# A recurrent layer on one core: the fifth mix matmul issued in turn with the first decay product, into other rows of the same PSUM bank

## The reference

```python
xn = _ln(x, ln1_w, ln1_b)
sx = _token_shift(xn, state[:, i1])                       # xn of the token before, minus xn
xxx = jnp.tanh((xn + sx * maa_x) @ maa_w1)                # 256 -> 5 * 32: the five mixes
xxx = jnp.matmul(xxx.reshape(b, l, 5, 1, 32), maa_w2)     # each 32 -> 256
x5 = xn[:, :, None] + sx[:, :, None] * (maa_stack + xxx)  # five modulated inputs
w = jnp.exp(-jnp.exp(time_decay + jnp.tanh(x5[:, :, 1] @ decay_w1) @ decay_w2))
r, k, v, g = x5[3] @ Wr.T, x5[0] @ Wk.T, x5[2] @ Wv.T, silu(x5[4] @ Wg.T)
# scan over tokens: out = r . (u * k v + s);  s = k v + w * s
# then a group norm, the gate, Wo, and a gated feed-forward with a token shift of its own
```

## Time and profile before

| what | us |
|---|---|
| median of 3 runs | 780.33 (779.73 to 785.28) |
| the profiled execution, its own time | 782.66 |
| its span in the trace | 780.9 |
| busy: PE / DVE / ACT / POOL | 670.8 / 647.7 / 367.4 / 269.7 |
| of it, pass from 495 to 560 us: PE / DVE / ACT / POOL | 58.1 / 63.1 / 30.4 / 31.0 of 65 |
| mean granted clock of PE over the span | 0.952 of full |

### The profile page before, as it was taken

How to read it: one execution, slowest core, us unless ns; L and a number is a source line. 1 busy time by engine, 2 the same in 40 slices (tenths; PEclk the granted TensorE clock), 3 DMA queues, 4 the chain that set the end, 5 groups by cost and what they waited for, 6 DMA issues and landing times.

```text
span 780.9 us, 9718 instructions
## 1 busy us (share of the span) xinstructions
PE 670.8 (86%) x2736; PEld 361.8 (46%) x2736; DVE 647.7 (83%) x983; ACT 367.4 (47%) x805; POOL 269.7 (35%) x192
## 2 busy tenths in 40 slices
PE   7789999979966978898988989898898988956887
PEld 5456666656422324253453435335344442514575
DVE  2499999973457799999999999999989999899623
ACT  3478888852241245346345244644615443352342
POOL 2840000000563363353626335354443633461000
PEclk9699999999998899999999999999999999997899
DMA  2611212200290443327055151514705332350000
GB/s 69 194 55 54 67 54 61 74 14 27 61 182 0 84 82 78 65 44 161 0 108 130 32 107 38 124 26 82 161 1 107 74 60 60 66 118 0 18 9 27
DMA packets 38298, 54.17 MB, mean 69 GB/s; under 512 B 4626, under 2 KB 21154, under 8 KB 38146
## 3 DMA queue, kind: packets, MB, share of 16 engines
q1 hardware_dynamic: 36866, 50.46, 28.8%
q0 software_dynamic: 1408, 3.43, 1.3%
HBM read 16.13 MB, written 4.19 MB: 26 GB/s over the span
## 4 chain that ended last, share of the span: by engine, by line
PE 29%; DVE 26%; issue 14%; ACT 3%; DMA 1%; POOL 1%; DVEq 1%; SPq 1%; POOLq 0%; ACTq 0%
DVE state L1174 13%; PE ps_a L733 6%; PE ps_a L746 4%; PE ps_a L762 4%; PE ps_c L819 4%; PE ps_c L733 3%; PE ps_a L771 2%; DVE x L1140 2%; PE ps_att L799 1%; DVE vb L1179 1%; DVE sx L1199 1%; DVE bonus L1148 1%; DVE st L1108 1%; ACT xn L1025 1%; PE ps_a L791 1%
## 5 line engine op out<-in xcount | busy, mean ns | idle before, releaser
L658 POOL TENSOR_TENSOR x<-x,xn 128x1024 f32<-128x1024 f32 x40 | 90.0, 2251 | 236.7 <-DVE x L1140 236.7
L1174 DVE TENSOR_TENSOR_SCAN state<-ps_w,state 128x512 f32<-128x512 f32 x128 | 145.8, 1201 | 9.2 <-ACT state L940 6.2
L733 PE MATMUL ps_a<-x,wsq 128*128 128x512 f32 x256 | 119.8, 610 | 11.1 <-ACT k L990 6.0
L653 POOL TENSOR_TENSOR state<-vb,k 128x2016 f32<-128x2016 f32 x24 | 114.3, 4761 | 41.9 <-ACT k L990 18.5
L1179 DVE TENSOR_TENSOR vb<-state,r 128x2048 f32<-128x2048 f32 x32 | 110.4, 3451 | 1.7
L1140 DVE SCALAR_TENSOR_TENSOR x<-ps_a,vec,sx 128x512 f32<-128x512 f32 x80 | 57.5, 745 | 42.2 <-PE ps_a L762 32.4
L733 PEld LDWEIGHTS ps_a<-x,wsq 128*128 128x128 f32 x256 | 47.9, 193 | 72.4 <-issue 55.7
L762 PE MATMUL ps_a<-mix_t,w 128*128 128x512 f32 x128 | 64.4, 618 | 14.9 <-DVE x L1140 14.9
L296 ACT ACTIVATE probs<-ps_f,negmax 128x256 f32<-128x256 f32 x128 | 58.8, 472 | 2.0 <-DVE negmax L345 1.2
L733 PE MATMUL ps_c<-zn,wsq 128*128 128x512 f32 x64 | 35.1, 699 | 17.4 <-DVE zn L1203 17.4
L345 DVE TENSOR_REDUCE negmax<-ps_f 128x2 f32<-128x512 f32 x64 | 41.2, 686 | 8.0 <-PE ps_f L218 5.6
(11 more groups left out here) (167 smaller groups left out, 1257.6 us busy)
## 6 DMA issues: line engine op xcount, KB each, us to landing
vb<-v SPq DMA_DIRECT2D x128, 256.0 KB, 5.8
x<-in_x SPq DMA_DIRECT2D x32, 128.0 KB, 2.1
c<-in_ctx SPq DMA_DIRECT2D x32, 128.0 KB, 2.1
x_chunk<-in_x SPq DMA_DIRECT2D x8, 512.0 KB, 7.4
out<-sx SPq DMA_DIRECT2D x8, 512.0 KB, 3.0
wsq<-in_wsq POOLq DMA_DIRECT2D x1, 1024.0 KB, 5.2
wsq<-in_wsq POOLq DMA_DIRECT2D x1, 768.0 KB, 6.8
s<-in_s POOLq DMA_DIRECT2D x1, 512.0 KB, 7.8
```

The lines of the kernel that those rows point to most:

```text
L653: nc.gpsimd.tensor_tensor(st[q][:, :, :, 1:L], src[:, :, :, 0:L - 1], wide(k[p][h][:, :])[:, :, :, 0:L - 1], ALU.mult).then_inc(kv_pool, 1)
L658: nc.gpsimd.tensor_tensor(x5[j % 2][:, :, :], x5[j % 2][:, :, :], xn[:, :, 1:L1], ALU.add).then_inc(x5_ready, 1)
L733: mm = nc.tensor.matmul(bank[:, :], wsq[:, weight, c, P * o:P * o + P], src(c), start=(c == 0), stop=(c == EC - 1))
L1174: nc.vector.tensor_tensor_scan(row, w[h][:, :], row, 0.0, ALU.mult, ALU.add).then_inc(scanned, 1)
```

## The change

Four things are altered.

1. `m1` leaves `a_mix` and the list `A_ORDER`. Its two matmuls are issued in `a_dec1`, in turn with those of `dec1`: m1 half 0, dec1 half 0, m1 half 1, dec1 half 1. They write rows 0 to 31 of the bank whose rows 64 to 127 take `dec1`.
2. The tanh of `m1` leaves `a_tanh` and stands behind the tanh of `dec1` in `a_dec`. Both count on `dec_tanh`, and all that reads `low_t` waits for the count of both.
3. `A_ORDER` has 24 names instead of 25. `T0`, `T1`, `g0` (of the next pass) and `w0a`, `w0b`, `w1a` now stand behind other readers of their banks; all other names follow the same one as before.
4. The passes are written out as separate functions instead of one with flags, a few helpers are added that are not used (`ADD_BY_VECTOR` is empty), `c_final` is cut in two functions called one behind the other, and a `memset` of `low_t` and one wait ahead of the drain stand some instructions elsewhere. The rest of the calls keeps its order.

```diff
-    A_ORDER = ["T0", "T1", "g0", "g1", "h0", "h1", "m0", "m1", "w0a", "w0b", "w1a", "w1b", "w2a", "w2b", "dec1",
-               "v0", "v1", "w3a", "w3b", "k0", "k1", "r0", "r1", "w4a", "w4b"]
+    A_ORDER = ["T0", "T1", "g0", "g1", "h0", "h1", "m0", "w0a", "w0b", "w1a", "w1b", "w2a", "w2b", "dec1", "v0",
+               "v1", "w3a", "w3b", "k0", "k1", "r0", "r1", "w4a", "w4b"]
...
-    A_READ = {"T0": (xn_ready, 1, 2), "T1": (xn_ready, 2, 2), "m0": (mix_tanh, 1, 2), "m1": (mix_tanh, 2, 2),
-              "dec1": (dec_tanh, 1, 1), "h0": (bonus_ready, 1, 2), "h1": (bonus_ready, 2, 2),
+    A_READ = {"T0": (xn_ready, 1, 2), "T1": (xn_ready, 2, 2), "m0": (mix_tanh, 1, 1),
+              "dec1": (dec_tanh, 2, 2), "h0": (bonus_ready, 1, 2), "h1": (bonus_ready, 2, 2),
...
             def a_mix(n):
                 pe.wait_ge(xm_ready, n * 2 + 2)
-                for name, lo, hi in (("m0", 0, P), ("m1", P, P + MIX)):
-                    bank = a_bank(n, name)
-                    for c in range(EC):
-                        mm = nc.tensor.matmul(bank[0:hi - lo, :], t["w1"][:, c, lo:hi], xm[:, TOK * c:TOK * c + TOK],
-                                              start=(c == 0), stop=(c == EC - 1))
-                    mm.then_inc(a_done, 1)
+                bank = a_bank(n, "m0")
+                for c in range(EC):
+                    mm = nc.tensor.matmul(bank[:, :], t["w1"][:, c, 0:P], xm[:, TOK * c:TOK * c + TOK],
+                                          start=(c == 0), stop=(c == EC - 1))
+                mm.then_inc(a_done, 1)
...
             def a_dec1(n):
-                pe.wait_ge(x5_ready, n * 5 + 1)
+                pe.wait_ge(*x5_at(n, 0))
                 bank = a_bank(n, "dec1")
                 for c in range(EC):
+                    nc.tensor.matmul(bank[0:MIX, :], t["w1"][:, c, P:P + MIX], xm[:, TOK * c:TOK * c + TOK],
+                                     start=(c == 0), stop=(c == EC - 1))
                     mm = nc.tensor.matmul(bank[DEC:2 * DEC, :], t["dw1"][:, c, :], x5_half(0)(c), start=(c == 0), stop=(c == EC - 1))
                 mm.then_inc(a_done, 1)
...
             def a_dec2(n, h):
 
-                pe.wait_ge(dec_tanh, n + 1)
+                pe.wait_ge(dec_tanh, n * 2 + 2)
...
             def a_tanh(n):
                 act.wait_ge(a_done, a_at(n, "m0"))
                 nc.scalar.activation(t1[:, :], ab("m0")[:, :], ACT.Tanh).then_inc(mix_tanh, 1)
-                act.wait_ge(a_done, a_at(n, "m1"))
-                nc.scalar.activation(low_t[0:MIX, :], ab("m1")[0:MIX, :], ACT.Tanh).then_inc(mix_tanh, 1)
...
                 nc.scalar.activation(low_t[DEC:2 * DEC, :], ab("dec1")[DEC:2 * DEC, :], ACT.Tanh).then_inc(dec_tanh, 1)
+                nc.scalar.activation(low_t[0:MIX, :], ab("dec1")[0:MIX, :], ACT.Tanh).then_inc(dec_tanh, 1)
```

More of the change, by code:

```diff
@@ new lines, in fill_pass @@
+            def fill_pass(n):
+                a_turn(n + 1)
+                warm(9)
+                a_mix(n + 1)
+                a_mod(n + 1, 0)
+                warm(2)
+                a_mod(n + 1, 1)
+                warm(1)
+                a_mod(n + 1, 2)
+                a_dec1(n + 1)
+                warm(2)
+                a_dec2(n + 1, 0)
+                a_proj(n + 1, 1, "v", WV)
+                a_mod(n + 1, 3)
+                a_proj(n + 1, 2, "k", WK)
+                a_proj(n + 1, 3, "r", WR)
+                a_mod(n + 1, 4)
+                a_dec2(n + 1, 1)
@@ new lines, in first_pass @@
+            def first_pass(n):
+                a_turn(n + 1)
+                a_proj(n, 4, "g", WG)
+                b_head_sum(n, 0)
+                b_head_sum(n, 1)
+                a_mix(n + 1)
+                a_mod(n + 1, 0)
+                a_mod(n + 1, 1)
+                b_reduce(n, 0, 0)
+                a_mod(n + 1, 2)
+                a_dec1(n + 1)
+                b_reduce(n, 0, 1)
+                b_bonus(n, 0)
+                a_dec2(n + 1, 0)
+                a_proj(n + 1, 1, "v", WV)
+                a_mod(n + 1, 3)
+                a_proj(n + 1, 2, "k", WK)
+                b_reduce(n, 1, 0)
+                a_proj(n + 1, 3, "r", WR)
+                a_mod(n + 1, 4)
+                b_reduce(n, 1, 1)
+                b_bonus(n, 1)
+                a_dec2(n + 1, 1)
@@ new lines, in body @@
+            def body(n):
+                a_turn(n + 1)
+                a_proj(n, 4, "g", WG)
+                c_var(n - 1)
+                b_head_sum(n, 0)
+                b_head_sum(n, 1)
+                a_mix(n + 1)
+                a_mod(n + 1, 0)
+                c_out(n - 1)
+                a_mod(n + 1, 1)
+                b_reduce(n, 0, 0)
+                a_mod(n + 1, 2)
+                a_dec1(n + 1)
+                b_reduce(n, 0, 1)
+                b_bonus(n, 0)
+                a_dec2(n + 1, 0)
+                a_proj(n + 1, 1, "v", WV)
+                c_turn(n - 1)
+                a_mod(n + 1, 3)
+                c_key(n - 1)
+                c_recept(n - 1)
+                c_value(n - 1)
+                a_proj(n + 1, 2, "k", WK)
+                b_reduce(n, 1, 0)
+                a_proj(n + 1, 3, "r", WR)
+                a_mod(n + 1, 4)
+                b_reduce(n, 1, 1)
+                b_bonus(n, 1)
+                a_dec2(n + 1, 1)
@@ new lines, in last_pass @@
+            def last_pass(n):
+                a_proj(n, 4, "g", WG)
+                c_var(n - 1)
+                b_head_sum(n, 0)
+                b_head_sum(n, 1)
+                c_out(n - 1)
+                b_reduce(n, 0, 0)
+                b_reduce(n, 0, 1)
+                b_bonus(n, 0)
+                c_turn(n - 1)
+                c_key(n - 1)
+                c_recept(n - 1)
+                c_value(n - 1)
+                b_reduce(n, 1, 0)
+                b_reduce(n, 1, 1)
+                b_bonus(n, 1)
@@ L1066, in body @@
[L1066 to L1078 removed]
+                c_x1(n - 1)
+                a_dec(n + 1)
+                state_column(n, 1, 0)
@@ L1089, in _, with drain_pass @@
+            def drain_pass(n, p):
+                q = 1 - p
+                c_rstd(n - 1)
+                c_x1(n - 1)
+                c_norm(n - 1)
+                c_xn2(n - 1)
+                c_kk(n - 1)
+                c_rr(n - 1)
             act.wait_ge(init_done, 3)
@@ new lines, in first_pass @@
+            def first_pass(n, p):
+                q = 1 - p
+                b_scan(n, p, 0, 0)
+                b_ruk(n, p)
+                a_shift(n + 1)
+                b_bonus(n, 0)
+                b_bonus(n, 1)
+                a_mod(n + 1, 0)
+                b_scan(n, p, 0, 1)
+                a_mod(n + 1, 1)
+                a_mod(n + 1, 2)
+                b_scan(n, p, 1, 0)
+                a_z(n + 2)
+                a_mod(n + 1, 3)
+                a_zm(n + 2)
+                b_kv(n, p, 1, 1)
+                b_scan(n, p, 1, 1)
+                a_mod(n + 1, 4)
@@ L1246, in body @@
+            def body(n, p, z=True):
+                q = 1 - p
+                b_scan(n, p, 0, 0)
+                b_ruk(n, p)
+                a_shift(n + 1)
+                b_bonus(n, 0)
+                b_bonus(n, 1)
+                c_gn(n - 1, q)
+                a_mod(n + 1, 0)
+                b_scan(n, p, 0, 1)
+                a_mod(n + 1, 1)
+                c_x1(n - 1)
+                a_mod(n + 1, 2)
+                b_scan(n, p, 1, 0)
+                c_shift(n - 1)
                 if z:
```

382 lines of the change are left out of this document (202 added, 180 removed).

## The result

The changed kernel takes 796.21 us (median of 4 runs, 792.4 to 799.06) beside 780.47 for the kernel before in the same comparison: a ratio of 1.0185, 95% interval 1.0126 to 1.0245. The forecast was 788.7 us with a range up to 794.0: the sign was right, and the loss was nearly twice as large, +14 to +16 us where +8.4 were forecast.

The account below looks back on a forecast made before the run. DVE was taken to set the length of a pass. Chunk 0 (1.35), five full chunks (5.10), chunk 6 (0.44) and chunk 1 (1.5) summed to 8.4 us more: 788.7 us, range 771 to 794.

Parts of the forecast that it names:

- The four matmuls run in a row: In `a_dec1`, the matmuls of `m1` and `dec1` run one after the other, 3.9 to 4.0 us; chance 0.74.
- 2.09 us for it: Price of the addition in `a_dec1`: `m1`'s 1.83 us plus 0.26 for two additional changes of width.
- The removal gives 1.07 a pass: Without `m1` behind `m0`, `w0a` starts 1.07 us earlier, all gained on the path by DVE.
- The sum: Over all chunks: 1.35 + 5.10 + 0.44 + 1.5 = 8.4 us more, median 788.7 us.
- The rival "the clock": Idle added behind `m0` brings three more half-clock spells of PE, 2.5 us each, making 796 us; chance 0.06.
- Pairs: Rival: `m1` runs beside `dec1` in `a_dec1`, the addition costs 0; 8.8 us less, 771.5 us; chance 0.16.
- half a pair: Rival: only weight loads or one half of each pair overlap, addition costs about 1, time stays at 780; chance 0.04.
- The moved tanh: On ACT behind `dec1`, 0.5 to 0.6 us ahead of the state column; hides by a hair, else 0.1 to 0.3 a pass.
- the banks: `w0a`, `w0b`, `w1a` and `T0` wait for other readers of their banks; all cost and give nothing.
- the chain of `xn2`: From `dec1` through `b_reduce` to `xn2`, it moves by the same 1.02 us, so nothing later absorbs the wait.
- chunk 0's tanh: In chunk 0's pass only a filler covers the moved tanh ahead of `a_dec2`, so 0.33 us are lost.

Follow-up runs that it names:

- e3_width32: Changed kernel with `dec1` cut into two tiles of 32 columns, so all tiles in the bank are 32 wide; 775.04 us, ratio 0.9939.
- e6_width64: Changed kernel with `m1` taken 64 columns wide, the width of `dec1`, its useful rows in 32 to 63; 776.05 us, ratio 0.9918.
- e4_grouped: Changed kernel with both matmuls of `m1` ahead of both of `dec1`, instead of in turn; 795.92 us, ratio 1.0127.
- e1_add: Kernel before, `m1` left in place and computed a second time in `dec1`'s bank (addition alone); 797.32 us, ratio 1.0232.
- e2_remove: Changed kernel without the two `m1` matmuls, its tanh still there (removal alone); 775.65 us, ratio 0.994.
- e7_fill: Changed kernel with filler matmuls in the full passes, one behind `m0` and four ahead of the head sums; 792.39 us, ratio 1.0142.
- e9_more_fill: Changed kernel with `dec1` in 32-wide tiles, five fillers per full pass, 12 more in chunk 1, 15 ahead of `c_out`; 768.08 us, ratio 0.9847.

## Why the prediction was right or wrong

- **The four matmuls run in a row: right.** 3.95 us measured, 3.9 to 4.0 forecast; DVE's wait for L811 2.26, forecast 2.2. The one place of the trace where both widths met (128*64 ahead of 128*32, an overlap of 0.07) was the right row to go by, and `attend`, which is closest in form, the wrong one: its tiles have one width. `e3_width32` and `e6_width64` show that the width decides it and not the bank, nor that the sources differ, nor the rows. The Trainium skill, TensorEngine Tiling (Array Packing), section "Key Properties", says that changing the tiling mode drains the TensorE and that different tiles work in parallel. By it the addition is serial here and free in `e3_width32`, and both traces agree (3.95 us in the change; starts within 0.01 us of each other at one width).
- **2.09 us for it: right.** 3.95 - 1.86 = 2.09, and `e4_grouped` gives 0.125 for each change of width, forecast 0.13. `e1_add` cost 17.5 us against 16.7.
- **The removal gives 1.07 a pass: right where the clock is full, and mis-sized in the sum.** In chunk 3 of the changed kernel DVE waits for nothing ahead of `w0a`. `e2_remove` was 7.8 us shorter between the marks against 7.7 forecast, by luck in part: less in most chunks, more in chunk 6. The removal alone is worth 4.2 us in the medians (1.7 to 7.6), not 8.8.
- **The sum is the step that failed.** It took every stretch at the granted clock that it had in the one trace, and carried only the spells that stood there (chunks 6 and 1) over. The changed kernel had others. Between the marks they cost 9.7 - 7.4 = 2.3 us in one execution, with one spell at `m0`, and 14.7 - 7.4 = 7.3 in the other, with two; `e7_fill`, with none, came out at +5.7 where the terms make +5.4. Behind chunk 7 they cost 2.0 to 2.3 us each time, ahead of the output product of the last pass, a stretch that no step of the forecast looked at; the profile of `e9_more_fill` shows this one. Added to +8.4 that makes +13 to +18, and +14.0 and +15.7 were measured. The attention, 3.9 and 4.9 us shorter in these two executions than in the profiled one of the kernel before, is left out of that sum: it differs between executions of every kernel here.
- **The rival "the clock" came true together with the forecast.** It had 796 us, the measured time, from three more spells of 2.5 us, and 0.06 of the chance. The number is luck: the profiled execution has one spell more at `m0`, at 3.7 us, the one in chunk 6 at its full price, and a longer half clock in chunk 1 and in the last pass. The argument against it, that the passes at a clock of 1.00 had the same idle and no spell, read one execution as if it were a property of the program. It was also priced as a case of its own, where every case should have had a term for it: with pairs the half clock is there too (a mean of 0.97 in each full pass of `e3_width32`), only cheaper, 0.3 to 0.5 us of wait ahead of `w0a`. Its reason, the idle time opened behind `m0`, isn't supported: a filler just there gained nothing.
- **Pairs, and half a pair: refuted here.** At one width the pairs do run, and the 8.8 us priced for them came out as 4.8 (`e3_width32`, 2.5 to 7.1) and 4.0 (`e6_width64`, whose interval of 3.4 to 9.4 still holds the 8.8). In the profile of `e3_width32` the passes gave theirs, 431.8 us between the marks against 440.9, and 2.1 went in the last pass.
- **The moved tanh, the banks and the chain of `xn2`: right in the full passes.** Nothing absorbed the wait, nothing new was late. For chunk 0's tanh 0.33 us were forecast, and DVE's wait ahead of `w3a` grew from 3.67 to 4.16.
